# Index copies on POOL: two columns ahead of each two gathers instead of 14 columns ahead of 14

## What is computed

```
edge_index = stack([src, dst])
h = maximum(layernorm(x), 0);  x = x + spmm(spmm(h))            # hops: weighted sums over edges, twice
h = maximum(layernorm(x), 0);  x = x + gcn(h)                   # sums over edges, scaled by degrees, times W
h = maximum(layernorm(x), 0);  x = x + gin(h)                   # h + sums over edges, two dense layers
h = maximum(layernorm(x), 0);  x = x + mpnn(h, edge_attr)       # messages from h[src], h[dst] and edge features
```

## Time and profile before

| | us |
|---|---|
| median of 3 runs | 5804.32 |
| lowest and highest | 5786.72, 5818.43 |
| profiled execution, first to last instruction | 5754.7 |
| its granted TensorE clock, mean | 0.722 |

### The profile page before, as it was taken

The page is one execution under the profiler, slowest core; times in us unless marked ns, Lnnn a source line. Parts: engine busy times, 40 slices in busy tenths (PEclk is TensorE's granted clock), DMA queues, the critical chain, the costliest instruction groups (busy, mean ns, idle before and its releaser), DMA issues. The chain is left out here.

```text
span 5754.7 us, 60611 instructions
## 1 busy us (share of the span) xinstructions
PE 3759.0 (65%) x18706; PEld 3006.2 (52%) x18706; DVE 3033.3 (53%) x7288; ACT 2016.3 (35%) x5132; POOL 3313.7 (58%) x2843
## 2 busy tenths in 40 slices
PE   3776666676999975565556777763566655666665
PEld 2544444446898964444445555553454444455454
DVE  4644444455556546665665766755454434455442
ACT  2444444451111113443444444431233333333332
POOL 4888888887888874444332554553444554445544
PEclk7776666675555557887888777875778877777787
DMA  8333333334444432222222333333121111121110
GB/s 293 51 51 51 51 51 51 51 42 73 87 81 87 87 40 82 78 93 79 96 77 75 108 125 123 112 107 130 54 91 55 59 57 57 54 91 55 60 54 21
DMA packets 335488, 452.10 MB, mean 79 GB/s; under 512 B 208111, under 2 KB 233301, under 8 KB 334740
## 3 DMA queue, kind: packets, MB, share of 16 engines
q1 hardware_dynamic: 159268, 361.69, 17.8%
q0 software_dynamic: 176000, 87.72, 12.5%
HBM read 258.41 MB, written 225.53 MB: 84 GB/s over the span
## 5 line engine op out<-in xcount | busy, mean ns | idle before, releaser
L929 POOL DMA_INDIRECT ga<-table,isl x784 | 783.9, 1000 | 278.1 <-issue 231.3
L1059 POOL DMA_INDIRECT out_x<-acc,osl x392 | 430.0, 1097 | 755.6 <-DVEq L80 640.4
L997 POOL DMA_INDIRECT xu<-acc,osl x392 | 625.1, 1595 | 144.6 <-issue 103.1
L1205 PE MATMUL tp<-xw,cc 128*128 128x394 f32 x784 | 411.5, 623 | 345.8 <-DVE cc L2011 215.4
L1242 PE MATMUL tp<-us,wide 128*128 128x64 f32 x1568 | 416.8, 422 | 87.4 <-DVE us L2139 49.2
L929 POOL DMA_INDIRECT ga<-xu,isl x392 | 394.0, 1005 | 121.5 <-issue 116.5
L1205 PEld LDWEIGHTS tp<-xw,cc 128*128 128x128 f32 x784 | 141.5, 220 | 603.1 <-issue 325.4
L1093 PE MATMUL mm<-ident,wide 128*128 128x128 f32 x1176 | 213.1, 343 | 355.6 <-DVE wide L2218 275.7
L1242 PEld LDWEIGHTS tp<-us,wide 128*128 128x128 f32 x1568 | 380.0, 332 | 92.2 <-DVE us L2139 49.4
L1255 PE MATMUL tp<-acc,wide 128*128 128x64 f32 x1560 | 423.3, 427 | 0.8
L1093 PEld LDWEIGHTS mm<-ident,wide 128*128 128x128 f32 x1176 | 180.0, 182 | 406.1 <-issue 323.2
(11 more groups left out here) (378 smaller groups left out, 9513.8 us busy)
## 6 DMA issues: line engine op xcount, KB each, us to landing
wide<-xu SPq DMA_DIRECT2D x84, 448.0 KB
zx<-key_rows SPq DMA_DIRECT2D x28, 896.0 KB
out_x<-wide SPq DMA_DIRECT2D x56, 448.0 KB, 3.4
table<-acc SPq DMA_DIRECT2D x56, 448.0 KB, 2.5
xf<-xs SPq DMA_DIRECT2D x56, 448.0 KB
wide<-table SPq DMA_DIRECT2D x56, 448.0 KB
xu<-in_x SPq DMA_DIRECT2D x25, 1000.0 KB
hop_even<-zeros SPq DMA_DIRECT2D x1, 12544.0 KB
```

Of the source, the lines that this page charges most:

```text
L929: nc.gpsimd.indirect_dma_start(o[:, g, :], None, table, bass.IndirectOffsetOnAxis(idx[:, g:g + 1], 0)).then_inc(s, 16)
L997: nc.gpsimd.indirect_dma_start(xu, bass.IndirectOffsetOnAxis(osl[b][:, g:g + 1], 0), acc[b][:, g, :], None, compute_op=ALU.add).then_inc(f ...
L1059: nc.gpsimd.indirect_dma_start(out, bass.IndirectOffsetOnAxis(osl[b][:, g:g + 1], 0), acc[b][:, g, :], None, bounds_check=nodes_max, oob_i ...
L1205: f.key_row.raise_by(nc.tensor.matmul(tp[1][:, at:at + KEYS], reach[:, g * P:g * P + P], key_steps, start=True, stop=True), ("g", b, g))
```

## The change

A new helper copies two index columns into their two columns of the slot, waits for this copy, and issues the two gathers that use them; it does so `HB` = 7 times for a unit. It replaces the copy of 14 columns and the 14 gathers in all places where POOL made them in this way: the first four units of the hops, both source phases, and all units of the last phase. In the last phase VectorE's copies of the slots (`next_slots`) are gone. `hop0`'s later gathers, all scatters, and the other engines' work are as before. The count of copies is carried along as `copied`.

```diff
+            def gather_by_pair(o, table, slot, index, c, s, copied):
+
+                for q in range(HB):
+                    slot_copy(slot[:, 2 * q:2 * q + 2], index[:, c + 2 * q:c + 2 * q + 2])
+                    after.wait_ge(s_slot, copied + q + 1)
+                    gather(o, table, slot, s, (2 * q, 2 * q + 1))
+                return copied + HB
...
             for u in range(4):
-                slot_copy(isl_of[u][:, :], dstc_i[:, u * G:u * G + G])
-                after.wait_ge(s_slot, base + u + 1)
-                gather(ga_of[u], x, isl_of[u], f.got[u])
+                copied = gather_by_pair(ga_of[u], x, isl_of[u], dstc_i, u * G, f.got[u], copied)
...
-                        slot_copy(isl[b][:, :], index[:, bass.ds(ecol(i, b), G)])
-                        after.wait_ge(s_slot, base + 2 * i + n + 1)
-                        gather(ga[b], table, isl[b], f.got[b])
+                        copied = gather_by_pair(ga[b], table, isl[b], index, ecol(i, b), f.got[b], copied)
...
-                    if first:
-                        slot_copy(isl[b][:, :], ptr_i[:, bass.ds(tcol(i, b), G)])
-                        after.wait_ge(s_slot, base + b + 1)
-                    gather(ga[b], tables[1], isl[b], tt.got_a[b])
+                    copied = gather_by_pair(ga[b], tables[1], isl[b], ptr_i, tcol(i, b), tt.got_a[b], copied)
...
                     for b in B2K:
-                        next_in = own.did(next_slots(j + 1, b))
-                        own.wait(tt.rows.at(j, ("us", b)), next_in)
+                        own.wait(tt.rows.at(j, ("us", b)))
                         tt.ga_free.raise_now(dve, ("g", b))
```

More of the change, by code:

```diff
@@ L930, in gather @@
                         o[:, g, :], None, table, bass.IndirectOffsetOnAxis(idx[:, g:g + 1], 0)).then_inc(s, 16)
+            def gather_by_pair(o, table, slot, index, c, s, copied):
[4 more added lines that the diff above has]
+                return copied + HB
             after.wait_ge(s_node, 1)
-            base = 0
+            copied = 0
             hop_max, all_max = pool.to_reg(ROWS + 4 * P - 1), pool.to_reg(ROWS + N + 4 * P - 1)
@@ L940, in _ @@
             for u in range(4):
-                slot_copy(isl_of[u][:, :], dstc_i[:, u * G:u * G + G])
-                after.wait_ge(s_slot, base + u + 1)
-                gather(ga_of[u], x, isl_of[u], f.got[u])
-            base += 4
+                copied = gather_by_pair(ga_of[u], x, isl_of[u], dstc_i, u * G, f.got[u], copied)
             def hop0(i):
@@ L1014, in _, with body @@
                         after.wait_ge(sp_[0].kept[b], 2 * 16 * STEPS)
-                def body(i, first):
-                    for n, b in enumerate(B2K if k == 0 else B2K[::-1]):
+                def body(i, first, copied):
+                    for b in B2K if k == 0 else B2K[::-1]:
                         if not first:
@@ L1023, in body @@
                                 after.wait_ge(*f.ga_free.at(i - 1, ("g", b)))
-                        slot_copy(isl[b][:, :], index[:, bass.ds(ecol(i, b), G)])
-                        after.wait_ge(s_slot, base + 2 * i + n + 1)
-                        gather(ga[b], table, isl[b], f.got[b])
+                        copied = gather_by_pair(ga[b], table, isl[b], index, ecol(i, b), f.got[b], copied)
+                    return copied
                 for i in range(STEPS):
-                    body(i, i == 0)
-                base += 2 * STEPS
+                    copied = body(i, i == 0, copied)
                 for b in B2K:
@@ L1040, in _, with t_gather @@
                 after.wait_ge(s_fixed, 32 * (k + 1))
-            def t_gather(i, first=False):
+            def t_gather(i, copied, first=False):
                 for b in B2K:
@@ L1064, in _ @@
                 after.wait_ge(s_dense[q], 16 * DSTEPS)
-            t_gather(0, True)
-            t_gather(1)
-            t_gather(2)
+            copied = t_gather(0, copied, True)
+            copied = t_gather(1, copied)
+            copied = t_gather(2, copied)
             t_scatter(0, True)
-            t_gather(3)
+            copied = t_gather(3, copied)
             for i in range(2, STEPS - 2):
                 t_scatter(i - 1)
-                t_gather(i + 2)
+                copied = t_gather(i + 2, copied)
             for i in (STEPS - 3, STEPS - 2):
@@ L2378, in _ @@
             descending = range(G - 1, -1, -1)
-            def next_slots(n, b):
-                n = 0 if isinstance(n, int) and n == STEPS else n
-                return V.tensor_copy(isl[b][:, :], ptr_i[:, bass.ds(tcol(n, b), G)])
             def last_pass(i, first=False, more_steps=True):
@@ L2649, in first_step @@
                 for b in B2K:
-                    next_in = own.did(next_slots(1, b))
-                    own.wait(tt.rows.at(0, ("us", b)), next_in)
+                    own.wait(tt.rows.at(0, ("us", b)))
                     tt.ga_free.raise_now(dve, ("g", b))
```

## The result

Changed kernel 5488.76 us (median of 4 runs, 5470.17 to 5507.66), kernel before 5811.38 (4 runs, 5786.72 to 5827.10): ratio 0.9447, interval 0.9413 to 0.9482. Faster, inside the range, but by 323 us where 666 were forecast. The two profiled executions differ by 5754.7 - 5484.4 = 270 us; the one of the kernel before is shorter than any of its four runs, and is not one of them.

A forecast was written before the change was run, and what follows sets the result against it. Bound by engines waiting for each other, TensorE's signals coming late during POOL's unbroken DMA rows. Savings of 121, 115, 410 and 20 us made 666, with the copies' cost off the path: 5804 - 666 = 5138, given as 5140; range 4880 to 5930.

The forecast's parts named there:

- The price: On POOL, 554 more copies at 0.18 us each: 100 us in all, 0 to 155 by the bounds.
- the cover of 46 us: Last phase: POOL's waiting per step, taken as cover for the copies' added 2.5 us per step.
- -121 and -115 forecast: Source phases 0 and 1: VectorE's "remote" waits shrink by 9.3 and 9.6 us per step, saving 121 and 115 us.
- The sign named for phase 0: Source phase 0: "remote" waits of L2208 and L2218 were to fall from 256 us to under 130.
- The start, -20 forecast: Hops' start: half of POOL's 40.1 us wait for its first rows goes, 20 us.
- The last phase: -410 forecast: Last phase: signals late by about 3 us cut the step from 123.0 to 82 us, 410 us over 10 steps.
- Rival 2: Closeness of DMAs counts and 1.25 to 1.34 us is a small step; a third of 666 returns: 5630 us, 13%.
- rival 1: Signals come on time altogether; POOL's floor of 77 us per step binds the last phase: 4900 us, 12%.
- Rival 3: VectorE still resumes only when a row of gathers ends, at L2208, L2218 and L2461; copies only add: 5920 us, 27%.
- the page's rule: DMA never contends with compute engines, TensorE and ScalarE wait for no one; by it only rival 3's price is left.

The follow-up runs named there:

- tiny_again: Kernel before plus a one-column POOL memset, and the wait for it, ahead of every second gather of each unit: 5701.4 us on chip 2, ratio 0.9914.
- quarter_pause: Kernel before plus an 80-column POOL memset and wait ahead of each whole unit's gather and each last-phase scatter: 4767.5 us on chip 13, ratio 1.0314.
- spaced_all: Kernel before plus a 448-column POOL memset and wait ahead of each whole unit's gather and each last-phase scatter: 5190.4 us on chip 11, ratio 1.1232.
- half_pause: Kernel before plus a 200-column POOL memset and wait ahead of each whole unit's gather and each last-phase scatter: 4888.9 us on chip 8, ratio 0.8497.

## Why the prediction was right and wrong

**What bounded the kernel: right, for the kind of chip that was profiled.** The late signals of the earlier trace rows were the cost, and the change gave part of it back.

**The price: 0.18 us a copy, 100 us in all.** Low. The copies from `ptr_i` take 246 ns on average, so 0.246 + 0.27 - 0.30 = 0.22 us, and those from `map_idx` 0.29. Net on a chip without late signals it is 4697.5 - 4624.7 = 73 us, most of it in the last phase (61 by the stages of chips 5 and 11), where the cover of 46 us of POOL waiting per step is gone and each step pays 4.9 us instead of the 2.5 reckoned. That cover existed only because of the late signals.
The Trainium skill, SBUF — State Buffer, "Who interferes with whom", says that a VectorE instruction with two SBUF inputs contends with a GpSimd one that reads SBUF. The trace agrees: of source phase 0's 196 copies, the 90 that overlap a VectorE instruction with two tensor inputs take 466 ns on average (up to 1151), the other 106 take 196 (at most 205). The one of 0.77 us at 2455.78 lies beside VectorE's L2201, `wide<-wide,st`, of 2455.42 to 2456.51.

**Source phases: -121 and -115 forecast, -98 and -168 measured (-93 and -191 on chip 2).** Sum 236 against 266 and 284: about right as a sum, but with some luck, since phase 0 was put too high and phase 1 a third too low. The sign named for phase 0 came true (L2208 and L2218 at 127.4 us, under 130). In phase 1 the prediction counted only L2218's 151.7 us. The same view has 52.0 us more of "remote" on VectorE (L2240 and L2208) and 181.6 on ScalarE; in the changed kernel (2962 to 3727 us) all of VectorE's are 61.4 and ScalarE's 31.1. The full steps of phase 1 fell from 61.6 to 47.7 us (46.9 on chip 2), near the 44.8 to 45.1 of chips without late signals. I think that VectorE's work, once it runs, slows POOL's gathers and so spreads them further. The gathers of phase 1 took 1109 ns on average (1042 before), and within a unit they start 1.52 us after each other (1.36 before), in source phase 0 1.49 (1.32 before), in the last phase only 1.36 (1.26 before). That is in line with it, but which of the two came first was not tested. The start, -20 forecast, gave 8 and 4.

**The last phase: -410 forecast, +3 and -44 measured. This is the step that failed**: "With a copy after every second gather a break comes each 0.95 + 0.30 + 0.95 + 0.48 = 2.7 us, so I take that a late signal is late by about 3 us". VectorE waited 47 us for L2457 through 14 breaks, and its signal was some 30 us late, not 3. The "remote" waits of that line went from 500.8 to 522.7 us, where under 150 were named, and the step from 123.2 to 124.6, where 82 was. The step took the break for the cause on one row, ScalarE's start 1.4 us after a copy. The run with as many breaks and hardly any distance (tiny_again) shows that short breaks give a sixth of the gain (0.9 of 5.1%). What the runs point to in its place is how far apart the DMAs are over the whole step: here the copies brought it from 1.27 to 1.32 us, where 1.36 gives 20 us per step and 1.50 all that POOL's pace allows. Distance was not told apart from the length of the break. That scatters "hardly hold TensorE" was read from one stretch too: spreading them by 0.09 us gave those 20 us.

**Rival 2 named the mechanism that fits the runs best**, given 13% and 5630 us: the distance and the small step. The time of 5489 us lies between it and the forecast's 5140. The rival erred in spreading "a third" evenly, since the source phases gave about what the forecast asked of them and the last phase next to none. I weighed its evidence, the second hop's 1.86 us, against rival 1 and not for rival 2. (That hop's first scatter starts at 1367 us, not at about 1220.)

**Rival 3 (5920) and the page's rule.** The Trainium skill, the same section, says that DMA never contends with a compute engine and that TensorE and ScalarE wait for no one. By it only the price was left. On the chips without late signals that is what happened (1.0154 on chip 5); on the others the traces do not agree with it, as far as a recorded execution can tell (see the last section). A profile of one chip could not show which kind it was.

**Rival 1's floor**, POOL's own 74.5 us per step of the last phase and 77 with the copies, is what binds on chips without late signals (76.2, and 81.1 with the copies).

## What to carry to other kernels

Where engines idle for late signals beside a dense row of DMAs, measure how the time depends on the mean distance of the DMAs before redesigning anything: a memset of 0.3 us ahead of each of 1232 gathers and 392 scatters gave 15% here, three times the change. Take the kernel to a second and third chip first, though; the same pause would by my estimate cost over 3% where signals are not late (quarter_pause 3.0 to 3.1%, spaced_all 12.3%). And a fix that works in two stages has to be priced in the third by that stage's own mean, scatters included.

## What the runs showed of the hardware

The same kernel takes 4622 to 4625 us on three chips and 5756 to 5811 on three other occasions, a fifth less, with nothing between. The hops are alike on both (first gather of source phase 0 at 2113 to 2127 us without late signals and at 2118 to 2133 with them); the difference lies in the three stages after them. POOL issues an indirect DMA in 0.95 to 0.98 us on both kinds, and VectorE's busy time agrees within 2 us (3032.3 and 3030.9 for the changed kernel). What differs is that TensorE's matmuls fall apart beside DMAs that are 1.25 to 1.35 us from each other. On the same chips the trace also lacks records: in the view of DMA issues (60 lines, of which 40 have a size) 3 rows of the changed kernel have a time to landing on the first chip and 22 on chip 5, and on chip 8 half_pause, with no late signal, has 3 as well. So it is in all traces: 2 to 5 rows on the first chip and chips 2 and 8, 22 to 25 on chips 5, 11 and 13. The changed kernel on the first chip:

```profile
zx<-key_rows SPq DMA_DIRECT2D x28, 896.0 KB
```

and on chip 5:

```profile
zx<-key_rows SPq DMA_DIRECT2D x28, 896.0 KB, 4.7
```

The Trainium skill, NOTIFIC — the notification-queue block, "3. Interfaces", says that this block, which writes the engines' event records, can stall an engine when an internal buffer fills. That the recording itself holds TensorE up on some chips would fit the missing records; it is a guess, no run here shows it, and since every time here comes with a recorded span, it was not tried. If it were so, neither the change nor the pauses would be worth anything in a run without a profile.
